# Layer norm applied by ScalarE with scale and shift, and a bias product moved to another bank, in a cross-attention and mixture-of-experts kernel

## The reference

```python
def _layernorm(x, axis=-1, eps=1e-05):
    m = jnp.mean(x, axis=axis, keepdims=True)
    v = jnp.var(x, axis=axis, keepdims=True)
    return (x - m) / jnp.sqrt(v + eps)

# cross-attention, 16 heads of 8; Q = _layernorm(x), K = V = ctx
q = Q @ Wq.T + bq;  k = K @ Wk.T + bk;  v = V @ Wv.T + bv      # then split into heads
A = einsum('bhqd,bhkd->bhqk', q, k) / sqrt(8)                  # causal: later keys are -inf
out = softmax(A) @ v                                           # heads joined again
x = x + out @ Wo.T + bo
# feed-forward with experts on xt = _layernorm(x)
shared = gelu(xt @ shared_up) @ shared_down                    # 2 shared experts of 64
gate   = softmax(xt @ router_w.T), the 4 largest of 16 kept
routed = sum over 16 experts of (gelu(xt @ up_r) * gate_r) @ down_r
x = x + shared + routed
```

## Time and profile before

| | |
|---|---|
| time, median of 3 runs (lowest to highest) | 215.53 us (215.24 to 215.61) |
| profiled execution: its time / its span | 215.19 us / 213.4 us |
| granted TensorE clock, mean | 0.998 |
| busy: PE / DVE / ACT / POOL | 185.1 (87%) / 170.2 (80%) / 141.7 (66%) / 96.6 us (45%) |
| share of the chain that ended last | PE 47%, DVE 18%, issue 9%, POOL 6%, ACT 6% |
| 16 applications of the first norm on DVE (line 724) | 6.0 us, mean 531 ns |
| 16 applications of the second norm on DVE (line 805) | 5.9 us, mean 410 ns |

### The profile page before, as it was taken

The page is one execution under the profiler, slowest core; times in us unless marked ns, Lnnn a source line. Parts: engine busy times, 40 slices in busy tenths (PEclk is TensorE's granted clock), DMA queues, the critical chain, the costliest instruction groups (busy, mean ns, idle before and its releaser), DMA issues.

```text
span 213.4 us, 4806 instructions
## 1 busy us (share of the span) xinstructions
PE 185.1 (87%) x1610; PEld 136.9 (64%) x1610; DVE 170.2 (80%) x456; ACT 141.7 (66%) x285; POOL 96.6 (45%) x184
## 2 busy tenths in 40 slices
PE   0539787998999899999999997899996989999991
PEld 0326564676677577767776774568884767677870
DVE  4667989978889999899899993349859759597881
ACT  4320265776778688766856778787787567968651
POOL 8559039948869676484575567601101010000000
PEclk9999999999999999999999999999999999999999
DMA  4474132742313313313213200100000001010001
GB/s 126 114 208 114 50 83 65 255 128 58 101 51 80 105 31 84 96 50 82 80 44 88 60 2 7 30 3 28 3 2 2 3 0 49 0 49 0 24 30 49
DMA packets 23736, 12.99 MB, mean 61 GB/s; under 512 B 4696, under 2 KB 23400, under 8 KB 23712
## 3 DMA queue, kind: packets, MB, share of 16 engines
q1 hardware_dynamic: 22288, 12.12, 20.5%
q10 hardware_dynamic: 1328, 0.53, 1.0%
q0 software_dynamic: 96, 0.03, 0.1%
HBM read 3.86 MB, written 1.05 MB: 23 GB/s over the span
## 4 chain that ended last, share of the span: by engine, by line
PE 47%; DVE 18%; issue 9%; POOL 6%; ACT 6%; DVEq 0%; ACTq 0%; POOLq 0%
DVE sb_mx L797 7%; PE psum L986 5%; PE psum L968 3%; PE psum L903 3%; PE psum L900 3%; PE psum L901 3%; PE psum L885 3%; PE psum L887 3%; PE psum L886 3%; PE psum L945 2%; POOL sb_probs L434 2%; PE psum L892 2%; PE psum L989 2%; POOL sb_x L441 2%; PE psum L952 2%
## 5 line engine op out<-in xcount | busy, mean ns | idle before, releaser
L597 ACT ACTIVATE sb_probs<-psum 128x512 f32<-128x512 f32 x96 | 55.8, 603 | 19.3 <-PE psum L968 18.3
L797 DVE TENSOR_REDUCE sb_mx<-psum 128x2 f32<-128x512 f32 (+1 forms) x96 | 62.5, 678 | 6.0 <-PE psum L952 3.6
L434 POOL TENSOR_SCALAR_AFFINE_SELECT sb_probs<-sb_probs 128x256 f32<-128x256 f32 (+1 forms) x96 | 45.3, 486 | 30.8 <-ACT sb_probs L597 29.9
L684 DVE TENSOR_TENSOR sb_probs<-sb_probs,psum 128x512 f32<-128x512 f32 x32 | 21.8, 682 | 10.9 <-ACT sb_probs L537 10.7
L537 ACT ACTIVATE sb_probs<-psum 128x512 f32<-128x512 f32 x36 | 21.4, 598 | 13.2 <-PE psum L887 13.0
L968 PE MATMUL psum<-sb_qk_op 128*128 128x256 bf16 x128 | 24.3, 272 | 2.2 <-DVE sb_bo L855 1.3
L945 PE MATMUL psum<-sb_qk_op 96*128 96x256 bf16 x128 | 25.7, 283 | 0.0
L691 DVE TENSOR_TENSOR sb_hid_l<-sb_probs,sb_hid_h 128x512 fp32r<-128x512 f32 x36 | 24.7, 686 | 0.3
L543 ACT CAST sb_hid_h<-sb_probs 128x512 fp32r<-128x512 f32 x36 | 22.2, 617 | 2.5 <-DVE sb_probs L684 2.3
L942 PE MATMUL psum<-sb_fut,sb_id_b 128*128 128x256 bf16 x64 | 18.2, 285 | 4.2 <-issue 3.6
L986 PE MATMUL psum<-sb_probs,sb_v_op 128*32 128x256 f32 x256 | 20.5, 391 | 1.2 <-ACT sb_o_raw L572 0.8
(11 more groups left out here) (114 smaller groups left out, 388.7 us busy)
## 6 DMA issues: line engine op xcount, KB each, us to landing
sb_qk_op<-sb_qk SPq DMA_DIRECT2D x90, 64.0 KB
sb_ctx<-in_ctx_t SPq DMA_DIRECT2D x8, 128.0 KB, 2.7
sb_num<-sb_o_raw SPq DMA_DIRECT2D x8, 128.0 KB, 2.1
out<-sb_o_raw SPq DMA_DIRECT2D x4, 256.0 KB, 2.3
sb_x<-in_x SPq DMA_DIRECT2D x3, 256.0 KB, 4.6
sb_up_f<-in_rup_t SPq DMA_DIRECT2D x1, 512.0 KB, 3.6
sb_dn_f<-in_rdown SPq DMA_DIRECT2D x1, 512.0 KB, 4.6
sb_qk_op<-sb_qk ACTq DMA_DIRECT2D x6, 64.0 KB
```

Of the source, the lines that this page charges most:

```text
L434: nc.gpsimd.affine_select(out=v, in_=v, compare_op=ALU.is_ge, fill=0.0, base=0, pattern=[[0, v.shape[1]], [1, P]], channel_multiplier=-1). ...
L597: nc.scalar.activation(probs[g][:, u * BANK:(u + 1) * BANK], psum[:, BANK_S + n % SB, :], ACT.Exp, scale=float(DH) ** -0.5).then_inc(s_exp, 1)
L684: nc.vector.tensor_tensor(hid[buf[k]], gel[buf[k]], psum[:, 3 + k % 2, :], ALU.mult)\
L797: nc.vector.tensor_reduce(dst, src, AX, ALU.max).then_inc(m_max, 1)
```

## The change

Three edits. The norm is now also written as one ACT instruction, x * rstd + shift with shift = -mean * rstd. It takes the place of the DVE instruction for parts 2, 3 and 4 of x (three times four tiles; parts 0 and 1 stay on DVE) and for all eight batches of the second norm (two tiles each). POOL makes the shift, with two more instructions in each of these places. On ACT the first-norm instructions stand at the units where they stood on DVE, but behind the projection's two ACT instructions; those of the second norm stand at t = 2 (t = 4 from turn 10 on) where DVE had them at t = 1 (t = 3). The product of the v bias goes to the bank of the sums (`BANK_PV`); the wait for `bo_done` moves from the first score product to the first weighted sum, and the wait for the transposed part 2 moves ahead of the bias product.

```diff
+        shift1 = sb("shift1", [P, NTT], F32)
+        shift2 = sb("shift2", [P, QB], F32)
...
+        def rstd_steps(q):
+            return 2 * (q + 1) if q < 2 else 4 * q
...
@@ POOL, rstd_1(q)
-                pool.wait_ge(rstd1, 2 * q + 1)
+                done = rstd_steps(q) - (2 if q < 2 else 4)
+                pool.wait_ge(rstd1, done + 1)
                 nc.gpsimd.tensor_tensor(rs1[:, tiles], var1[:, tiles], halfs[:, tiles], ALU.pow).then_inc(rstd1, 1)
+                if q >= 2:
+                    pool.wait_ge(rstd1, done + 2)
+                    nc.gpsimd.tensor_tensor(shift1[:, tiles], mv1[:, tiles, 0], rs1[:, tiles], ALU.mult).then_inc(rstd1, 1)
+                    pool.wait_ge(rstd1, done + 3)
+                    nc.gpsimd.tensor_scalar(shift1[:, tiles], shift1[:, tiles], -1.0, None, ALU.mult).then_inc(rstd1, 1)
@@ POOL, turn_of, t == 0
                         nc.gpsimd.tensor_tensor(rs2[:, :], var2[:, :], halfs[:, 0:QB], ALU.pow).then_inc(rstd2, 1)
+                        pool.wait_ge(rstd2, 4 * c + 2)
+                        nc.gpsimd.tensor_tensor(shift2[:, :], mv2[:, :, 0], rs2[:, :], ALU.mult).then_inc(rstd2, 1)
+                        pool.wait_ge(rstd2, 4 * c + 3)
+                        nc.gpsimd.tensor_scalar(shift2[:, :], shift2[:, :], -1.0, None, ALU.mult).then_inc(rstd2, 1)
@@ ACT
+            def apply_1(q):
+                act.wait_ge(rstd1, rstd_steps(q))
+                for a in range(*X_PARTS[q]):
+                    nc.scalar.activation(xn[:, a, :], x2[:, a, :], ACT.Identity, bias=shift1[:, a:a + 1],
+                                         scale=rs1[:, a:a + 1]).then_inc(xn_done, 1)
...
+                    if t == late(turn, 2) and c is not None:
+                        act.wait_ge(rstd2, 4 * c + 4)
+                        for a in range(QB):
+                            nc.scalar.activation(xn2[:, a, :], x2[:, c * QB + a, :], ACT.Identity, bias=shift2[:, a:a + 1],
+                                                 scale=rs2[:, a:a + 1]).then_inc(xn2_done, 1)
+                    if (turn.at, t) in ((1, 4), (2, 1), (3, 1)):
+                        apply_1(turn.at + 1)
@@ DVE, turn_of
-                    if t == late(turn, 1) and c is not None:
-                        dve.wait_ge(rstd2, count(2 * c + 2))
-                        for a in range(QB):
-                            nc.vector.tensor_scalar(xn2[:, a, :], x2[:, bass.ds(c * QB + a, 1), :].rearrange("p a e -> p (a e)"),
-                                                    mv2[:, a, 0:1], rs2[:, a:a + 1], ALU.subtract, ALU.mult)\
-                                .then_inc(xn2_done, 1)
...
-                    if (turn.at, t) in ((1, 4), (2, 1), (3, 1)):
-                        apply_1(turn.at + 1)
...
-                    nc.vector.tensor_tensor(bo_sb[:, :], bo_sb[:, :], psum[:, BANK_S, 0:E], ALU.add).then_inc(bo_done, 1)
+                    nc.vector.tensor_tensor(bo_sb[:, :], bo_sb[:, :], psum[:, BANK_PV, 0:E], ALU.add).then_inc(bo_done, 1)
@@ PE, exp_unit
-                if (c, t) == (0, 0):
-                    pe.wait_ge(bo_done, 1)
@@ PE, pv
+                if (c, g) == (0, 0):
+                    pe.wait_ge(bo_done, 1)
@@ PE, end of turn 1
-                    mm(psum[:, BANK_S, 0:E], bv_all[:, :], wo_sb[:, :], start=True, stop=True).then_inc(bv_ps, 1)
+                    pe.wait_ge(xnt_read, 3)
+                    mm(psum[:, BANK_PV, 0:E], bv_all[:, :], wo_sb[:, :], start=True, stop=True).then_inc(bv_ps, 1)
                     pe.wait_ge(ones_in, 32)
-                    pe.wait_ge(xnt_read, 3)
```

More of the change, by code:

```diff
@@ L463, in turn_of @@
                         nc.gpsimd.tensor_scalar(var2[:, :], mv2[:, :, 1], 1e-5, None, ALU.add).then_inc(rstd2, 1)
-                        pool.wait_ge(rstd2, count(2 * c + 1))
+                        pool.wait_ge(rstd2, 4 * c + 1)
                         nc.gpsimd.tensor_tensor(rs2[:, :], var2[:, :], halfs[:, 0:QB], ALU.pow).then_inc(rstd2, 1)
+                        pool.wait_ge(rstd2, 4 * c + 2)
+                        nc.gpsimd.tensor_tensor(shift2[:, :], mv2[:, :, 0], rs2[:, :], ALU.mult).then_inc(rstd2, 1)
+                        pool.wait_ge(rstd2, 4 * c + 3)
+                        nc.gpsimd.tensor_scalar(shift2[:, :], shift2[:, :], -1.0, None, ALU.mult).then_inc(rstd2, 1)
                     if t == 10 and c is not None and turn.at < NB + 2:
@@ L799, in turn_of @@
                             split_maxima(c, turn.side(1), t // 6)
-                    c = turn.batch(4)
-                    if t == late(turn, 1) and c is not None:
-                        dve.wait_ge(rstd2, count(2 * c + 2))
-                        for a in range(QB):
-                            nc.vector.tensor_scalar(xn2[:, a, :], x2[:, bass.ds(c * QB + a, 1), :].rearrange("p a e -> p (a e)"),
-                                                    mv2[:, a, 0:1], rs2[:, a:a + 1], ALU.subtract, ALU.mult)\
-                                .then_inc(xn2_done, 1)
                     if (turn.at, t) == (0, 9):
@@ L836, in turn_of @@
                         dve.wait_ge(x2_done, count(c + 1))
-                        dve.wait_ge(rstd2, count(2 * c))
+                        dve.wait_ge(rstd2, 4 * c)
                         for a in range(QB):
```

## The result

The changed kernel takes 222.55 us (median of 4 runs, 221.23 to 223.92), the kernel before beside it 215.57 us (215.24 to 216.82): 1.032 times as long [1.028, 1.035]. The profiled execution has a time of 221.23 us and a span of 219.1 us, 5.7 us more than before, where the sum said 5.35.

A forecast was written before the change was run, and what follows sets the result against it. PE was taken to bound the attention turns at 14.34 us each; 0.37 + 0.33 + 3.7 + 0.25 + 0.1 + 0.6 = 5.35 us on 215.19 us gave 220.5 us. Its own range was 219 to 222, the stated range 217.3 to 222.6.

The forecast's parts named there:

- the prediction's 0.03: At the second norm's transposes: behind a true wait the next PE instruction follows some 0.03 us closer, taken off PE's loss.
- +0.37 at 42.30: Head, at PE's sum at 42.30 waiting for the last mask: -0.36 + 0.13 + 0.6 us for POOL's two new instructions.
- +0.33: Turn 3: PE's transposes of part 4 lose 1.29 us, less 0.96 us that PE was idle further on.
- the 0.96 us that the prediction took off for the wait further on: Turn 3: PE's idle time at 50.04 for DVE, set against the 1.29 us lost at part 4's transposes.
- +0.25: Turn 9, where ACT is full: two applications add 0.73 us, less 0.48 us idle ahead of reading the transposes.
- +0.1: Turns 10 and 11 together: applications ahead of a gelu with 0.51 us to spare; little of the rest reaches PE.
- +0.6 in full: Start of turn 11: POOL's pair for the shift delays the gates, for which PE is already idle 1.30 us.
- the stated range: 217.3 to 222.6 us, from the cheap case at the low end to the dear case at the high end.
- DVE sets the pace: Rival: DVE's lead of 0.79 us a turn lets PE run without waits; -2.5 us, 212.7 us; chance 7%.
- Cheap: Rival on ACT's price: two applications of the second norm take 0.42 us; +2.2, 217.4 us; chance 13%.
- dear: Rival on ACT's price: applications at 0.57 and 0.47 us, 1.04 for two; +7.4, 222.6 us; chance 6%.
- No change: Rival: the stalls fall into waits PE now has elsewhere, beyond 1.75 us of turns 4, 6, 7; 215.2 us; 4%.

The follow-up runs named there:

- the transposes at t = 4: Bias edit and part 2 on ACT, plus second norm on ACT, its transposes at t = 4, gates ahead of the shift's pair in turn 11: 215.76 us.
- the kernel with rstd behind the mask: Changed kernel with POOL's four instructions for part 4 of the first norm behind the last mask of batch 0 instead of ahead: 220.24 us.
- the parts measured apart: Changed kernel with second norm back on DVE, 216.52 us; with first norm back on DVE, 219.49 us; kernel before with bias edit alone, 215.11 us.
- the run without the second norm: Kernel before without applying the second norm on any engine, PE transposing x itself, statistics and rstd kept: 215.29 us.
- part 2 on ACT: Kernel before with the bias edit and only part 2 of the first norm on ACT, parts 3 and 4 and second norm on DVE: 213.71 us.

## Why the prediction was right, point by point

*The turns.* The mechanism held at the place predicted. Predicted for turns 4 to 8: 0.0, +1.33, +0.81, +0.59, +0.99, or 3.7 us. Measured by the start of PE's sum of each turn: -0.09, +1.25, +0.71, +0.50, +1.13, or 3.5 us. Two small errors cancel. The applications land 0.05 us later than estimated. And turn 5 of the kernel before was not free of waits, as the prediction had it: its last transposes of the maxima start 0.37 us behind the score product ahead of them, in the changed kernel 0.23 (the end of turn 5 before, and of turn 4 after):

```profile
85.93 0.38 PE L968 MATMUL psum<-sb_qk_op 128*128 128x256 bf16 x2
86.30 0.27 PE L1000 MATMUL psum<-sb_id_b,sb_m_parts 128*128 128x128 bf16 x2
```

```profile
73.02 0.38 PE L985 MATMUL psum<-sb_qk_op 128*128 128x256 bf16 x2
73.25 0.27 PE L1019 MATMUL psum<-sb_id_b,sb_m_parts 128*128 128x128 bf16 x2
```

The difference is DVE's, by my reading: its second split takes 0.48 us there instead of 0.17 and its addition to x ends at 86.15 us, as in turn 4 on a smaller scale.

In turn 4 the transposes of the norm start 4.10 us into the turn where they started 2.97 us into it, 1.13 us later. At the gates it is still 1.10 us, so the prediction's 0.03 was right; the turn ends 0.96 us later than PE's 14.34 us, since 0.14 us fall into that small wait.

*Turn 4* came out as predicted, but for a reason that I had not seen. I took the 1.05 us beyond PE's own work as room. It was one PE wait of 1.02 us for DVE's addition, late by two stretched splits of the maxima. In the changed kernel, and in the six others in which ACT's norm stands at t = 2, the splits at the turn's end take 0.17 us each, so that wait is gone while ACT's has come. With the transposes at t = 4 turn 4 lasts 14.75 us against 15.37 with the norm on DVE. That POOL, whose mask and product run from 70.05 to 71.44 us in the kernel before, stretches DVE's splits of 70.28 to 71.48 is a reading of the timelines: POOL is at work beside the splits that take 0.41 to 0.43 and 0.73 us (four traces compared), and idle, or within 0.1 us of it, beside those that take 0.17 (the changed kernel: POOL idle from 71.66 to 72.54, splits from 72.14 to 72.52; four traces compared). No run moved POOL's work alone.

*The head.* "+0.37 at 42.30" measured +0.66. The steps: the pair of POOL 0.59 (predicted 0.6), POOL's idle time gone -0.36 (-0.36), but the mask behind ACT's part 3 starts 0.39 us later and not 0.13. ACT's four applications take 1.54 us to the next start instead of 1.46, and the turn began 1.1 us earlier, not 1.33, since PE now waits 0.81 us for the splits of the maxima.

*Turn 3.* "+0.33" measured +0.72; this term missed its mechanism. The loss at the transposes was replaced by a low clock for 3.4 us. In the kernel with rstd behind the mask, where the clock held, PE waits 1.24 us at the transposes of part 4 (predicted: 1.29). But the 0.96 us that the prediction took off for the wait further on did not come off: 0.91 us of that wait are left, and turn 3 lasts 16.43 us there, from a sum that starts 1 us earlier, against 15.02 before.

*Turns 9 and 10.* "+0.25" and most of "+0.1" did not come: from the start of turn 9 to PE's last wait for the gates the changed kernel is 0.04 us longer. PE waits in turn 9 for the same exponentials as before (0.30 and 0.75 us in both).

*Turn 11.* "+0.6 in full" measured 0.91 (1.30 to 2.21 us). The pair is 0.61 of it; the rest is the second instruction of the split of the gates, which takes 0.57 us where it took 0.25:

```profile
170.69 0.22 POOL L465 CAST sb_g_parts<-sb_gate 128x32 fp32r<-128x32 f32 x1
171.00 0.57 POOL L467 TENSOR_TENSOR sb_g_parts<-sb_gate,sb_g_parts 128x32 fp32r<-128x32 f32 x1
```

It is so in every kernel with the pair ahead of the gates (waits of 2.19 to 2.21 us), and not in those without. The pair shifts it to another moment, and what runs beside it there seems to be what stretches it. In all six traces where it takes 0.57 or 0.58 us, DVE at that moment subtracts two tiles of SBUF into `hid_l`; in the eight where it takes 0.25, DVE multiplies by a bank of PSUM. The row of the changed kernel:

```profile
170.76 0.69 DVE L720 TENSOR_TENSOR sb_hid_l<-sb_probs,sb_hid_h 128x512 fp32r<-128x512 f32 x1
```

*The median.* The sum was made against a profiled execution and came within 0.4 us of one, in part by luck: turns 2 and 3 cost 1.38 us against 0.70 and turn 11 0.91 against 0.6, and the terms of turns 4 to 10 were too high by about 0.5 us together. The median is 2 us above the forecast, outside its own range of 219 to 222 and inside the stated range by 0.05 us. The prediction has no term for that. The mean clock of the runs of 222.31 (0.992) and 222.79 us (0.990) is that of the profiled execution (0.991), which had one fall; only that of 223.92 us (0.983) leaves room for a second. Three things on record have the size of what is left: a second fall (1.57 us at the gates), a fall at the gates in place of the one at the mask (1.57 against 0.45), and a late start of some 1.2 us (last section). The longer runs have no trace, so which of them it was stays open, and so do the 1.6 us that the parts measured apart leave.

*The rivals.* "DVE sets the pace" fell with the run without the second norm. "Cheap" and "dear" were settled by 0.49 us for one application and 0.88 for two (theirs were 0.42 and 1.04 for two). That the median meets the 222.6 of "dear" is chance; besides, the terms given for it (5.35 + 5 x 0.22 + 2 x 0.4 + 0.5) make +7.75 and not +7.4. "No change" never had a case in turns 5 and 8.

*Two things I would have got wrong beyond the forecast:* that ACT has room once the transposes stand later (it is 0.4 us late each turn, and its idle time elsewhere in the turn does not help), and that a gain of 1.3 us from the bias edit would be there by itself: alone it is 0.5 us (215.11 against 215.59 us), not clear of the noise, and 1.8 us together with part 2 on ACT.

## What to carry to other kernels

An instruction moved to the engine with more idle time is paid for at the place where it is queued: compare, at that one place, when its consumer comes with when the new engine can have finished, and then ask which instruction stands behind it and how many banks lie between that and the engine that sets the pace. A busy share of 66% said that ACT had room; it had none between the projection and the exponentials. An earlier place is paid for by what then stands behind it. Small instructions on an idle engine count in full where one thing waits for them, and a wait of the matmul engine that grows by a few tenths may cost its clock as well: look at the granted clock by the microsecond behind the longest waits, and at all runs and not at the profiled one.
